# A decoder's causal attention: scores masked and reduced in one VectorE pass per head, written to SBUF

## What is computed

```python
q = (x @ Wq).reshape(b, t, HKV, G, HD)
k = (x @ Wk).reshape(b, t, HKV, HD)
v = (x @ Wv).reshape(b, t, HKV, HD)
scores = jnp.einsum('bqhgd,bkhd->bhgqk', q, k) / jnp.sqrt(jnp.float32(HD))
scores = jnp.where(jnp.tril(jnp.ones((t, t), bool)), scores, NEG)
attn = jax.nn.softmax(scores, axis=-1)
ctx = jnp.einsum('bhgqk,bkhd->bqhgd', attn, v).reshape(b, t, HQ * HD)
return ctx @ Wo
```

## Time and profile before

| | us |
|---|---|
| median of 3 runs | 1022.23 |
| the three runs | 1019.52, 1022.23, 1023.61 |
| the profiled execution | 1014.81 |
| its span | 1013.1 |
| PE busy in the span | 922.9 (91%) |
| DVE busy in the span | 770.7 (76%) |
| ACT busy in the span | 622.0 (61%) |
| POOL busy in the span | 510.8 (50%) |

### The profile page before, as it was taken

One profiled execution on the slowest core, in us unless ns is written; L12 is line 12 of the kernel. 1 busy time (PEld: TensorE's weight loads), 2 busy tenths in 40 slices (PEclk: granted clock), 3 DMA queues, 4 the chain that ended last, 5 costly groups with the idle time before them and its releaser, 6 DMA issues. The chain is left out here.

```text
span 1013.1 us, 19520 instructions
## 1 busy us (share of the span) xinstructions
PE 922.9 (91%) x6196; PEld 477.5 (47%) x6196; DVE 770.7 (76%) x1660; ACT 622.0 (61%) x1496; POOL 510.8 (50%) x845
## 2 busy tenths in 40 slices
PE   3899999999999998899979999999999999898496
PEld 1322222222233334565645555565555655577396
DVE  7899899889999986899836677666766756686464
ACT  4488888888888884233256565656566565354154
POOL 7266666776454453110045455545555454585444
PEclk8699999999999999999989999999999999996598
DMA  5099930000000000000070000000000000000240
GB/s 105 1 232 246 249 73 1 2 1 2 2 1 0 0 1 1 1 1 1 0 216 7 9 7 14 9 7 9 7 14 9 6 1 1 2 1 17 94 120 20
DMA packets 50699, 37.68 MB, mean 37 GB/s; under 512 B 15737, under 2 KB 48677, under 8 KB 50608
## 3 DMA queue, kind: packets, MB, share of 16 engines
q1 hardware_dynamic: 48864, 32.83, 13.6%
q0 software_dynamic: 1744, 3.72, 1.1%
HBM read 15.54 MB, written 21.45 MB: 37 GB/s over the span
## 5 line engine op out<-in xcount | busy, mean ns | idle before, releaser
L725 DVE TENSOR_REDUCE a_nmax<-a_rows 128x2 f32<-128x1024 f32 x256 | 299.7, 1219 | 24.3 <-PE a_rows L439 21.5
L979 ACT ACTIVATE a_probs<-a_turned 128x512 f32<-128x512 f32 x512 | 270.0, 605 | 46.8 <-PE a_turned L465 45.5
L1510 POOL TENSOR_TENSOR a_prob<-a_prob,a_rinv 128x256 f32<-128x256 f32 (+3 forms) x128 | 159.6, 1253 | 162.9 <-DVE a_rinv L1772 162.4
L1765 DVE TENSOR_REDUCE a_nmax<-a_score 128x2 f32<-128x256 f32 (+3 forms) x128 | 105.3, 823 | 107.4 <-PE a_score L1560 104.1
L1686 ACT ACTIVATE a_prob<-a_score,a_nmax 128x128 f32<-128x128 f32 (+3 forms) x256 | 132.5, 523 | 86.7 <-DVE a_nmax L1765 86.3
L465 PE MATMUL a_turned<-a_q,a_qk 32*128 32x512 bf16 x512 | 136.4, 388 | 7.4 <-ACT a_probs L979 5.0
L424 PE MATMUL a_acc<-a_probs,a_vg 128*32 128x512 f32 x1024 | 137.2, 608 | 0.2
L439 PE MATMUL a_rows<-a_qk 32*128 32x512 bf16 x512 | 108.8, 397 | 5.9 <-DVE a_nmax L725 4.3
L465 PEld LDWEIGHTS a_turned<-a_q,a_qk 32*128 32x128 bf16 x512 | 34.9, 91 | 153.0 <-ACT a_probs L979 124.7
L1557 PE MATMUL a_score<-a_k_s,a_q_s 64*128 64x384 f32 (+3 forms) x512 | 103.7, 481 | 2.9 <-ACT a_prob L1686 1.3
L1778 DVE COPY a_pt<-a_turn 128x128 f32<-128x128 f32 (+3 forms) x224 | 92.1, 447 | 1.4 <-PE a_turn L1571 1.4
(11 more groups left out here) (361 smaller groups left out, 1590.7 us busy)
## 6 DMA issues: line engine op xcount, KB each, us to landing
xs_sorted<-a_blank SPq DMA_DIRECT2D x9, 1935.0 KB
m_m_w<-L_ffn_w SPq DMA_DIRECT2D x8, 512.0 KB, 8.4
c_xs<-xs_sorted SPq DMA_DIRECT2D x23, 129.0 KB, 2.1
g_a_wq<-L_attn_Wq SPq DMA_DIRECT2D x32, 64.0 KB, 2.0
g_X<-x SPq DMA_DIRECT2D x4, 256.0 KB, 4.8
a_wgu<-L_ffn_gate_up_proj SPq DMA_DIRECT2D x1, 1024.0 KB, 5.5
a_wdn<-L_ffn_down_proj SPq DMA_DIRECT2D x1, 512.0 KB, 6.8
g_a_wk<-L_attn_Wk SPq DMA_DIRECT2D x8, 64.0 KB, 1.8
```

The lines of the kernel that those rows point to most:

```text
L725: dve.tensor_reduce(nmax[i % 2][:, p // 2, (p % 2) * 2:(p % 2) * 2 + 2], rows[n % 2][:, :, :], AX_X, ALU.max, negate=True).then_inc(row_ou ...
L979: act.activation(probs[:, (tb % 2) * 4 + j, :], turned[n % 3][:, :], ACT.Exp, scale=float(HD0) ** -0.5).then_inc(turn_out, 1)
L1510: pool.tensor_tensor(pr, pr, spread(rinv[:, t % RING, :], 2, width), ALU.mult).then_inc(scl, 1)
L1765: dve.tensor_reduce(nmax[:, t % RING, :], score[t % 2][:, :, 0:width], AX_X, ALU.max, negate=True).then_inc(mx, 1)
```

## The change

The mask becomes a float32 tile `past_mask` of 128 by 512, zero but for its last 128 columns, which hold the triangle; the last `width` columns of it are the mask of a block. TensorE's mask products go. VectorE's reduction over both heads becomes one `tensor_tensor_reduce` per head: it reads the scores from PSUM and the mask from SBUF, adds them, negates, writes the result to `prob` in SBUF, and keeps the minimum, which is the negated maximum. ScalarE takes the exponential of `prob` in place, with scale -1. The semaphores go with it: the scores count heads (2 per item), `mx` counts heads, the scores of t wait for the maxima of t - 2 in place of the exponentials, and the wait for the transposes of t - 4 moves from ScalarE to VectorE, ahead of the pass. VectorE waits once for the mask at the stage's start, where TensorE did.

```diff
-        causal = sc.sb("causal", [P, P], BF16)
+        past_mask = sc.sb("past_mask", [P, S], F32)
...
-            pool.memset(causal[:, :], 0.0).then_inc(cz, 1)
+            pool.memset(past_mask[:, :], 0.0).then_inc(cz, 1)
             pool.wait_ge(cz, 1)
-            pool.affine_select(out=causal[:, :], in_=causal[:, :], compare_op=ALU.is_ge, fill=-1e30, base=0,
-                               pattern=[[-1, P]], channel_multiplier=1).then_inc(cz, 1)
+            pool.affine_select(out=past_mask[:, S - P:S], in_=past_mask[:, S - P:S], compare_op=ALU.is_ge, fill=-1e30,
+                               base=0, pattern=[[-1, P]], channel_multiplier=1).then_inc(cz, 1)
...
-            pe.wait_ge(cz, 2)
...
-                wait(pe, ex, 2 * (t - 1) + 2 * ALL_IT * r)
+                wait(pe, mx, 2 * (t - 1) + 2 * ALL_IT * r)
...
-                              k_s[i // 2 % 2][h, 0:width], start=True, stop=False)
-                for j in range(2):
-                    last = pe.matmul(score[t % 2][:, j, sb * P:width], g.ident16[:, :], causal[:, :],
-                                     start=False, stop=True)
-                last.then_inc(s_s, 1)
+                              k_s[i // 2 % 2][h, 0:width], start=True, stop=True).then_inc(s_s, 1)
...
-                act.wait_ge(mx, t + 1 + ALL_IT * r)
-
-                wait(act, tps, 2 * (t - RING + 1) + 2 * ALL_IT * r)
                 for j in range(2):
-                    act.activation(prob[t % RING][:, j, 0:width], score[t % 2][:, j, 0:width], ACT.Exp,
+                    act.wait_ge(mx, 2 * t + j + 1 + 2 * ALL_IT * r)
+                    act.activation(prob[t % RING][:, j, 0:width], prob[t % RING][:, j, 0:width], ACT.Exp, scale=-1.0,
                                    bias=nmax[:, t % RING, j:j + 1], accum_out=rsum[:, t % RING, j:j + 1]).then_inc(ex, 1)
...
             ln.vector_norm(dve, (B - 1,))
+            dve.wait_ge(cz, 2)
...
-                dve.wait_ge(s_s, t + 1 + ALL_IT * r)
-                dve.tensor_reduce(nmax[:, t % RING, :], score[t % 2][:, :, 0:width], AX_X, ALU.max,
-                                  negate=True).then_inc(mx, 1)
+                wait(dve, tps, 2 * (t - RING + 1) + 2 * ALL_IT * r)
+                for j in range(2):
+                    dve.wait_ge(s_s, 2 * t + j + 1 + 2 * ALL_IT * r)
+                    dve.tensor_tensor_reduce(out=prob[t % RING][:, j, 0:width], in0=score[t % 2][:, j, 0:width],
+                                             in1=past_mask[:, S - width:S], scale=-1.0, scalar=3e38, op0=ALU.add,
+                                             op1=ALU.min, accum_out=nmax[:, t % RING, j:j + 1]).then_inc(mx, 1)
```

## The result

| us | before | after |
|---|---|---|
| median | 1020.88 (4 runs) | 1005.45 (4 runs, 1004.42 to 1009.01) |
| ratio, with its 95% interval | | 0.987 (0.984 to 0.990) |
| a second timing, ratio | 1017.98 (17 runs) | 1006.57 (6 runs); 0.9895 (0.986 to 0.993) |
| the profiled execution | 1014.81 | 1009.01 |
| attention stage in the trace | 343.46 | 334.41 |

What follows compares the result with a forecast made beforehand. TensorE was taken to bound the attention stage; 0.12 - 0.05 = 0.07 us for each of 128 items makes 9.0 us, and 1022.2 - 9.0 = 1013 us, with a range of 1004 to 1024 us.

Steps and rivals of the forecast that it cites:

- TensorE sets the stage: Attention stage: TensorE busy 332.9 of 337.3 us, everyone waits for it, so the stage shrinks by the work it loses.
- The mask products: TensorE, attention stage: 0.12 us per item less 0.05 given back, 0.07 us times 128 items, 9.0 us gained.
- the exposed load of the transposes: Transposes on TensorE: their first float32 weight load no longer runs beside mask products; 0.05 us charged to every item.
- The fused pass: VectorE, attention stage: 1.04 ns an element, 0.15 to 0.29 us more an item, 19 to 37 us in all, covered.
- The accumulator's read: VectorE, second instruction after each fused pass: costs between 0 and 0.07 us per head, the trace row nearest to 0.
- The margin: Step with 128 and 256 keys: VectorE's copies end 0.27 us before transposes need the bank; afterwards 0.06 to 0.20, no stall.
- The other edits: Moved waits count nothing; ScalarE's SBUF source 0.03 us times 256, 7.7 us, covered; GpSimd's memset about 0.52 us, covered.
- Given back: Rival, chance 0.22: exposed load or VectorE stalls, 6 us of the 9, take back TensorE's gain; about 1019 us.
- Half rate: Rival, chance 0.12: VectorE's fused pass takes two cycles an element, 85 us more; stage about 361 us, total 1046 us.
- the point of decision: Half rate on VectorE: the pass's rate decides the stage from about 1.6 cycles an element on.
- Contention: Rival, chance 0.04: fused passes slow down while GpSimd multiplies, adding 143 us to VectorE; 1072 us.
- the base: Whole kernel: 1022.2 us, the median of three runs, 7.4 us above the profiled execution, from which the gain was subtracted.

Runs made afterwards that it cites:

- e1: The kernel before without its mask products on TensorE, reduction and exponentials as they were; stage 333.29 us against 343.46, ratio to before 0.989.
- e2: The changed kernel with the mask products kept on TensorE, so the mask is added twice; stage 343.97 us, ratio to before 1.000.
- v2: The changed kernel with the first head's copy of the 256 key blocks moved from VectorE to ScalarE; stage 333.24 us against 334.41.
- m1: The changed kernel with one spare fused pass of 128 columns ahead of the real one in every item; stage 343.42 us against 334.41.
- m3: The changed kernel with a spare fused pass over three quarters of the columns ahead of the real one for every head; stage 373.69 us against 334.41.
- e4: The changed kernel with 14 spare 512-wide fused passes from SBUF, six at the stage's start and eight in units; stage 334.78 us against 334.41.

## Why the prediction was right, step by step

**TensorE sets the stage: shown.** Taking its mask products alone gives 10.17 us (e1), the rest alone gives nothing (e2).

**The mask products: slightly undersized.** 0.07 us an item and 9.0 in all were forecast, 0.079 and 10.2 measured. The 0.05 us for the exposed load of the transposes is there in all but one of the steps with four of them (0.66 against 0.61). One place near the stage's end had to stand for all steps; the rows of after put the steps between 0.07 and 0.09 us.

**The fused pass: right in its price, too dear in its step.** 686 and 287 ns against 680 and 287 reckoned. But I added durations, and instructions overlap: an item costs 0.09 us more on VectorE from start to start at 128 keys (0.06 at 512 in the place looked at), not 0.15 to 0.29, and VectorE's sum rose by 11 us, not 19 to 37. The accumulator's read hides under the next start, the end of the bound that the earlier trace rows lay nearest to.

**The margin: this step failed.** I reckoned 0.06 to 0.20 us, "thin, but no stall"; it is some 0.05 us less than nothing in most of the 256 key steps (0.68 us from scores to transposes, against 0.63). I compared the end of the second copy with the second head's transposes; the first copy comes first, and between the middle of the pair and the transposes' start pass 0.18 us, which I left out. With them, give 711.08 - 710.77 - 0.18 = 0.13 us before the change, not 0.27. The error cost only some 1.1 us, as v2 shows, which takes the copy away and gains them. It cost so little because the pass was cheaper than reckoned, and that was luck; m1 shows what 0.2 us more would have cost.

**The other edits.** The waits that were moved cost nothing that e2 could show. ScalarE got 32 ns dearer at full width, for 30 reckoned, and stayed covered. GpSimd's memset took 0.52 us and its idle time behind it shrank from 0.62 to 0.30, as worked out:

```profile
512.84 0.52 POOL L1459 MEMSET a_past_mask<- 128x512 f32 x1 [12.34 <-POOLq L62]
...
514.11 0.23 POOL L124 TENSOR_SCALAR a_ln_ve<-a_ln_mv 128x4 f32<-128x4 f32 x1 [0.30 <-DVE a_ln_mv L118]
```

**The rivals.** *Given back* came in small: 1.1 of 10.2 us, and not the 6 of 9 that it had. *Half rate* did not come, and its price of 361 us was too low: m3 bears about the same load and takes 367.4 us in the prediction's count. I let 32 us of VectorE's idle time stay, and in that count it kept 51. The load is not spread as the waits are: what counts is each step, not the sum. For the same reason the point of decision was wrong: m1, with 24.6 us more on VectorE than the changed kernel, already gives back the whole gain. The Trainium skill ("Vector Engine (DVE) Microarchitecture Reference", section 7) says that the form `S2S2D2_STT` has its throughput halved with two sources in SBUF that are not bf16. For `tensor_tensor_reduce`, which the trace shows as a custom operation, no run here shows that: 0.69 us at 512 wide from two float32 sources in SBUF, the same as from PSUM. *Contention* is real for two SBUF sources (1.79 us) and absent with one in PSUM.

**The number.** 1013 us against 1005.45. The stage has no share in the 7.6 us: 9.0 us were forecast for it and 9.05 came, but as 10.2 from the mask products less 1.1 for the margin, two errors that cancel by luck. 1.3 us are the base: the runs shown had 1022.2 as their median, all four runs 1020.9. The rest, some 6 us, is a difference that the stage does not show. In the second timing most of what lies beyond the stage goes with the granted clock, as said above; for the first that is likely but not shown. That the whole difference of 15.4 us equals the upper end of 0.12 us times 128 is chance, as the stage gained 9.05.

## What to carry to other kernels

Price a removed matmul from start to start of what surrounds it, not by its own duration: 256 products of 224 ns were worth 10 us. Where the work goes to an engine with a third of its time idle, look for the step in which that engine hands a buffer back, and measure the margin from the end of the hand-over to the start of the taker, latency included. An engine that is 71% busy over a stage can have no slack in one step out of four, and there an added 0.2 us is paid in full (m1), while 14.4 us put behind the last item of a unit, ahead of its wait for the next scores, cost 0.4 (e4).

## What was not expected of the hardware

The fused pass and the read of its accumulator (82 ns) let the next instruction start together with that read, so the read costs nothing from start to start. The same pass with both sources in SBUF took 0.69 us beside GpSimd's memsets and selects, and 1.79 us when GpSimd's multiplication had begun before it.
